# One load of 128 partitions in place of four of 32 for the turned squares of an attention and mixture-of-experts block

## The reference

```python
q, k, v = split_heads(x @ Wq), split_heads(x @ Wk), split_heads(x @ Wv)   # 16 heads of 64
q, k = apply_rope(q), apply_rope(k)
sim = einsum('bid,bjd->bij', q, k) * 64 ** -0.5
attn = softmax(where(causal, sim, -inf))
x = layernorm(x + einsum('bij,bjd->bid', attn, v) @ Wo + bo)
w, i = top_k(softmax(x @ gate_w.T + expert_bias), 2)                      # 8 experts
y = sum over the two experts of weight * (gelu(x @ w_up[e].T) @ w_down[e].T)
x = layernorm(x + layernorm(y) + x)
```

## Time and profile before

| | us |
|---|---|
| three runs, median | 805.34 |
| three runs, lowest and highest | 800.24, 806.1 |
| the profiled execution | 798.51 |
| its span, first to last instruction | 796.7 |
| TensorE busy in it | 755.9 |
| VectorE busy | 667.4 |
| ScalarE busy | 592.2 |
| GpSimd busy | 572.0 |

### The profile page before, as it was taken

One profiled execution on the slowest core, in us unless ns is written; L12 is line 12 of the kernel. 1 busy time (PEld: TensorE's weight loads), 2 busy tenths in 40 slices (PEclk: granted clock), 3 DMA queues, 4 the chain that ended last, 5 costly groups with the idle time before them and its releaser, 6 DMA issues.

```text
span 796.7 us, 20539 instructions
## 1 busy us (share of the span) xinstructions
PE 755.9 (95%) x5763; PEld 535.0 (67%) x5763; DVE 667.4 (84%) x2514; ACT 592.2 (74%) x1678; POOL 572.0 (72%) x701
## 2 busy tenths in 40 slices
PE   8899999999999999999999989999998899999995
PEld 4455666666666566666666656666656579999995
DVE  6688888999899879998999899989987974235997
ACT  3688878878878777877887768777877756565677
POOL 3686767558765877677768886976786266989983
PEclk9999999999999999999999999999999999999998
DMA  4576666456755566556555655565557667434525
GB/s 152 188 224 200 214 203 201 165 191 197 227 180 174 174 200 195 188 180 210 175 186 191 194 173 186 186 199 173 177 179 225 222 193 207 109 85 125 163 90 163
DMA packets 110719, 144.66 MB, mean 182 GB/s; under 512 B 13392, under 2 KB 86352, under 8 KB 110608
## 3 DMA queue, kind: packets, MB, share of 16 engines
q1 hardware_dynamic: 106240, 134.49, 53.8%
q0 software_dynamic: 4224, 8.72, 3.3%
q10 hardware_dynamic: 144, 0.13, 0.1%
HBM read 61.42 MB, written 45.17 MB: 134 GB/s over the span
## 4 chain that ended last, share of the span: by engine, by line
PE 67%; POOL 13%; DVE 8%; issue 7%; DMA 3%; ACT 1%; SPq 0%; DVEq 0%; POOLq 0%; ACTq 0%
PE AO L1109 15%; PE S_all L1068 14%; PE TB L1089 9%; PE AO L1129 5%; PE S_all L1256 4%; POOL yrows L956 4%; PE TB L1269 2%; POOL shared L973 2%; PE AO L1269 2%; DVE Sm L1609 2%; DMA qk<-shared 2%; DVE x_acc L1630 1%; PE TB L1000 1%; POOL shared L722 1%; PE TB L998 1%
## 5 line engine op out<-in xcount | busy, mean ns | idle before, releaser
L1376 ACT ACTIVATE Pr_all<-Sm,nmax 128x512 f32<-128x512 f32 (+3 forms) x512 | 281.8, 563 | 23.7 <-DVE nmax L1609 22.9
L1609 DVE CUSTOM_DVE_ANT_0 Sm<-S_all,causal 128x512 f32<-128x512 f32 (+3 forms) x512 | 223.0, 482 | 46.0 <-PE S_all L1068 45.9
L1068 PE MATMUL S_all<-qk 64*128 64x512 f32 (+3 forms) x1024 | 169.8, 446 | 10.9 <-DVE nmax L1609 8.6
L717 POOL TENSOR_TENSOR qk<-shared,qk 128x512 f32<-128x512 f32 x64 | 81.9, 1280 | 129.6 <-DMA qk<-shared 119.9
L1109 PE MATMUL AO<-PT,shared 128*64 128x128 f32 x1008 | 149.6, 438 | 13.1 <-issue 12.7
L1386 ACT ACTIVATE PT<-TB 128x768 f32<-128x768 f32 x189 | 107.8, 605 | 61.2 <-PE TB L1089 61.2
L1630 DVE SCALAR_TENSOR_TENSOR x_acc<-AO,rinv,x_acc 128x128 f32<-128x128 f32 x504 | 141.7, 344 | 3.5 <-POOL x_acc L769 1.3
L1068 PEld LDWEIGHTS S_all<-qk 64*128 64x128 f32 x1024 | 79.7, 187 | 82.6 <-issue 56.9
L1089 PE MATMUL TB<-ident,Pr_all 128*128 128x128 f32 x764 | 109.2, 279 | 3.6 <-ACT PT L1386 3.1
L1089 PEld LDWEIGHTS TB<-ident,Pr_all 128*128 128x128 f32 x764 | 82.0, 141 | 44.4 <-issue 40.6
L1109 PEld LDWEIGHTS AO<-PT,shared 128*64 128x64 f32 x1008 | 66.5, 136 | 61.1 <-issue 30.9
(11 more groups left out here) (335 smaller groups left out, 1459.0 us busy)
## 6 DMA issues: line engine op xcount, KB each, us to landing
turns<-turned_pr SPq DMA_DIRECT2D x63, 512.0 KB
PT<-turns SPq DMA_DIRECT2D x252, 128.0 KB
qk<-shared SPq DMA_DIRECT2D x124, 256.0 KB
wo<-in_wo SPq DMA_DIRECT2D x64, 64.0 KB, 3.1
PT<-yrows SPq DMA_DIRECT2D x7, 512.0 KB, 4.3
w_tile<-in_wup SPq DMA_DIRECT2D x10, 256.0 KB, 3.5
xt<-xrows SPq DMA_DIRECT2D x32, 65.0 KB, 2.7
x_acc<-in_x SPq DMA_DIRECT2D x8, 256.0 KB, 3.4
```

The lines of the kernel that those rows point to most:

```text
L717: nc.gpsimd.tensor_tensor(qT[p][:, :], q_cos, qT[p][:, :], ALU.add).then_inc(q_ready, 1)
L1068: nc.tensor.matmul(SB[2 * (group % 2) + h][:, at:at + (qb + 1) * P], qT[p][half, qb * P:qb * P + P], kT[p][half, 0:(qb + 1) * P], start=Tr ...
L1376: nc.scalar.activation(Pr[j][:, 0:n], Sm[j], ACT.Exp, bias=nmax[:, j:j + 1], scale=-1.0, accum_out=rsum[p][:, h * QB + qb:h * QB + qb + 1] ...
L1609: nc.vector.tensor_tensor_reduce(out=Sm[j], in0=SB[2 * (group % 2) + h][:, at:at + n], in1=causal[:, T - n:T], scale=-0.125, scalar=HUGE, ...
```

## The change

The store writes partition a*32 + r of `turned_pr` into DRAM row 4r + a, in place of row 32a + r. The rows that one partition of `PT` needs (r fixed, a from 0 to 3) then stand side by side, so that the pair (r, a) is a single dimension with one step, and all four groups b can be named in one transfer of three dimensions. The four transfers become one of 512 KB on 128 partitions, and `LOADED` becomes 16. As two loads in flight would now share one semaphore's count, the load waits first for the load before it.

```diff
-LOADED = LANES * 16
+LOADED = 16
...
                 sp.wait_ge(turned, 2 * u + 2)
                 wait(sp, turns_in, LOADED * (u - 1))
-                sp.dma_start(turns[p * P:p * P + P, :], turned_pr[:, :, :, :].rearrange("p b c s -> p (b c s)")).then_inc(stored, 16)
+                sp.dma_start(turns[p * P:p * P + P, :].rearrange("(r a) n -> a r n", a=LANES),
+                             turned_pr[:, :, :, :].rearrange("p b c s -> p (b c s)")).then_inc(stored, 16)
 
             def load_turned(u, p):
 
                 sp.wait_ge(stored, 16 * (u + 1))
+                wait(sp, turns_in, LOADED * u)
                 wait(sp, pv_done, u - 1)
-                squares = turns[p * P:p * P + P, :].rearrange("(a r) (b n) -> b r a n", r=SQ, b=LANES)
-                for b in range(LANES):
-                    sp.dma_start(PT[p][SQ * b:SQ * b + SQ, LANES * (QB - 1):, :, :].rearrange("k a c s -> k a (c s)"),
-                                 squares[b]).then_inc(turns_in, 16)
+                squares = turns[p * P:p * P + P, :].rearrange("(r a) (b n) -> b (r a) n", a=LANES, b=LANES)
+                sp.dma_start(PT[p][:, LANES * (QB - 1):, :, :].rearrange("k a c s -> k (a c s)"), squares).then_inc(turns_in, 16)
```

## The result

The changed kernel takes 1220.14 us (median of four runs, 1212.31 to 1234.0) against 803.05 us for the kernel before on the same chip: ratio 1.519, 95% interval 1.508 to 1.530. The 1234.0 us is an execution in the chip's slower state, which ratio and interval leave out. The forecast was 1052 us with a range of 950 to 1180. The direction was right, and the size was not: the change costs some 417 us where 246 + 8 were worked out.

A forecast was written before the change was run, and what follows sets the result against it. TensorE's matmul stream bound the kernel before; afterwards the queue on four DMA engines would, at 13.8 us a unit. The profiled 798.5 us plus 246 for 61 units and 8 for the later start gave 1052 us, range 950 to 1180.

The forecast's parts named there:

- how the transfers are dealt: New store and load: outermost DRAM dimension 4 puts each on four of 16 DMA engines; both narrow had chance 0.78.
- what would show it: Signs in the profile: attend spacing near 14 us, DMA share near 0.4, TensorE idle 4 us a unit before line 1109.
- the store's term: Store of the turned squares, issue to landing: 2.66 us plus 3.82 for four engines, 6.5 us.
- The load's term: Single load of the turned squares on four engines, issue to landing: 8.7 us.
- The queue sum: Packets queued on the four DMA engines per unit: store 5.10, load 5.85, swap and others 2.8, together 13.8 us.
- the loop: Two units pass while attend-to-store time, store and load pass: (9.6 + 6.5 + 8.7)/2 = 12.4 us a unit.
- the slow rate: Load on four engines at 16.8 GB/s each: 7.8 us in place of 5.85, giving 15.7 us a unit, 1175 us.
- X: From the start of one attend to the issue of the store two units on: taken as 9.6 us.
- decides only from about 14 us of work on: Rival, TensorE's clock falls: hidden by the queue unless work per unit reaches about 14 us; 1350 us throughout; chance 0.03.
- Sixteen engines: Rival: store and load still use 16 DMA engines, about 8 us saved before attend, 790 us; chance 0.08.
- one transfer alone: Rival: only load or only store on four engines, 848 us (load) or 829 us (store); chance 0.08.
- hidden: Rival: SP's waits for VectorE or another stall take each freed stall's place, 798 to 805 us; chance 0.03.

The follow-up runs named there:

- the dose of 16, 8 and 4: Kernel before with the added wait, only the store's outermost DRAM dimension set to 16, 8 or 4: ratios 1.017, 1.094 and 1.158.
- e3_wide_both: Changed kernel's row order and added wait, but store and load each in four transfers of 32 partitions: 815.36 us, 1.012 of the kernel before.
- e7_wait_alone: Kernel before with only the added wait for the load of the unit before: 807.43 us, ratio 1.001.
- e1_narrow_store: Changed kernel's store (outermost dimension 4), with its load as four transfers of 32 partitions: 1090.57 us, 1.353 of the kernel before.
- s4_four_parts: Kernel before with the added wait, store in four transfers of outermost dimension 4, each engine reading 8 neighbouring partitions: 933.88 us, ratio 1.158.
- e9_after_small_swap: Changed kernel with its rotary swap transfers cut to 128 of 1024 columns: 1201.46 us, 1.492 of the kernel before.
- f1_after_filled: Changed kernel with 60 small matmuls put before TensorE's wait for the load in each unit: 1212.78 us, 1.517 of the kernel before.
- g2_dealt_by_exp: Kernel before with block 3's exponential reading scores in steps of 4, so one load of outermost dimension 128 suffices: 796.26 us, 0.992.
- g1_dealt_keys: Kernel before with block 3's score matmuls reading keys in steps of 4, and one load of outermost dimension 128: 830.22 us, 1.037.

## Why the prediction was right and wrong

**Right: how the transfers are dealt.** The step that decided the direction took four engines for an outermost dimension of 4, without a row that showed such a transfer. The stretches of after (112 GB/s at a share of 0.28, 95 at 0.30), the landings in 4 pieces, the dose of 16, 8 and 4, and the 1.012 of both transfers kept wide all bear it out. The rule of the count that the prediction quotes from the Trainium skill held. The other one quoted there, one transfer of 128 partitions in place of several, is given on that page for transfers that use all 16 engines. The load of this change doesn't, and takes 9.5 us where four of 32 partitions take 5.2.

**Right: the parts at no cost.** Row order in itself (`e3_wide_both`, 1.2% at most with its four-part stores), the added wait (`e7_wait_alone`, 1.001), three issues fewer (SP waits for the store in 62 of 63 units).

**Right in part: what would show it.** DMA share 0.37 and 0.39 for "near 0.4"; SP waits for the store in 62 of 63 units; store issue to load issue over 6.5 us. GB/s fell by two fifths (195 to 115), not by a third; TensorE's stall is 322.6/62 = 5.2 us a unit, not 4; the spacing is 16.4, not 14. All off in one direction.

**Wrong: the store's term, "2.66 + 3.82 = 6.5".** It measured 11.2 us in after and 10.2 with wide loads. The rate of one engine was taken from sixteen, whose packets of 4 KB took 161 ns in the mean, and the four engines of the change read partitions 32 apart, where a packet takes 273 (`e1_narrow_store`). With engines that read 8 neighbours each the same store takes 7.7 us in `s4_four_parts`, at 193 ns a packet. The last 1.0 us of after comes with the narrow load: store and load are in flight together there, in four pieces each. The load's term, 8.7, measured 9.5, near enough.

**Wrong: which of the two sums.** The queue sum (13.8) was chosen over the loop (12.4) as the larger one. `e9_after_small_swap` refutes it as the pace. That it brought the forecast nearer to the result, 1052 against 967 by the loop, is luck. (The upper end given for the slow rate, 1175, is 1168 by its own terms, 798.5 + 8 + 61 x 5.93.) The loop's form holds, and its inputs didn't: (9.6 + 6.5 + 8.7)/2 = 12.4 became (12.0 + 11.2 + 9.5)/2 = 16.4. Over two units the store's term brings 4.7 us of the 8 that are missing, X 2.4, the load 0.8. The 61 units from unit 1 to unit 62 then take (1057.64 - 59.37) - (636.16 - 40.45) = 402.6 us more. The start was mis-sized as well: `attend` of unit 1 comes at 59.4 us where it was 40.5, 18.9 us later in place of 8. These two, and 5 us more behind the `attend` of unit 62, are the 426 us between the two profiled spans (1223.1 and 796.7); the medians differ by 417.

**Wrong: X was held at 9.6.** It had been read in a kernel in which SP and TensorE wait little. The timeline of after shows two things that lengthen it. `attend` at 414.76 runs at 1.2 GHz for 4.54 us in place of 2.37, and VectorE comes to its transposes 10.98 us after it (425.74), where it was 8.27 in before (300.90 - 292.63). And the transposes at 437.96 waited for the store before, were done at 439.27, but their store was issued at 440.88 only: SP had been held by the wait for that store until 437.53 and then had a load of `wo` and one of `x_acc` to issue, 2.6 us with the gaps. With the store at 10 us this one-unit loop alone (store, then what SP or VectorE does before the next) asks for 13.5 to 14 us, as `e1_narrow_store` shows. Of the `wo` load and the store behind a wait on SP the prediction had said, for the added wait alone, "which it would hold by the same nothing", and it didn't ask the same of the wait for the store. It also wrote of the clock that it "decides only from about 14 us of work on". That compares the clock with all of TensorE's work in a unit, but the clock fell to 0.82 and 0.80, and a slow `attend` can lengthen X however much room the rest has. What part of X's 2.4 us is the clock's is not settled: X is 0.9 us shorter in the profiled execution of `f1_after_filled`, but the fill takes time as well, and the kernel is no faster.

**The rivals.** Sixteen engines, one transfer alone and hidden are refuted. When one transfer alone is made narrow, it costs 286 us (store) and 188 us (load), where the rivals' prices were 24 and 43. The store's is the mis-sized term again, with the one-unit loop behind it. For the load the term was near (9.4 measured, 8.7 taken), but the store of before doesn't stay at 2.7 beside it (4.7, as four transfers), and X goes from 9.6 to 10.7: (10.65 + 4.73 + 9.44 + 0.4)/2 = 12.6 for the 10.5 worked out.

## What to carry to other kernels

Before merging transfers, write both sides' access patterns down and look at the outermost dimension. Here the one large transfer with 128 on both sides (`g2_dealt_by_exp`) was faster than four small ones, and the one with 4 on the DRAM side was slower; for the store 16 was already 1 us slower than 128. Where the layout doesn't give it, change the order of data in an instruction of an engine that has room (here the exponential's read: 66 us more on ScalarE, and none of it in the time of the kernel). And when a term of a loop is to double, don't keep the other terms: read which instruction stands behind the new wait on its queue, and which buffer has only one copy.

## What the runs showed of the hardware

- **Which partitions are read at one time matters, at the same count of engines.** 512 KB on four engines: 7.7 us when each engine reads 8 neighbours and the four start 8 apart, 10.2 when they start 32 apart. On sixteen engines with 8 neighbours each: 3.9 us against 2.9 of before, packets of 262 ns in the mean against 161.
- **A step of 4 in an fp32 operand is not free.** As moving operand of the score matmul over 512 columns: 640 to 1101 ns (`before` and `g1_dealt_keys`, the longest block, in which alone the operand is stepped). In ScalarE's exponential over 512 columns: 714 to 1233 ns.
- **TensorE lost its clock at stalls of a few microseconds.** After 8.00 us of idling `attend` took 4.54 us at a granted clock of 0.50, which is 1.2 GHz; after 2.47 us of idling it took 2.37.
- **A narrow store took longer beside a narrow load.** After's store takes 11.2 us where it takes 10.2 beside wide loads; with the store in four parts it is 9.4 against 7.7. The narrow load stays at 9.4 to 9.6 us beside either kind of store.
